# A new opening for a two-layer attention and expert kernel: order and size of the loads, the first two units ahead of the beats, the input norms moved to ACT

## The reference, cut to what matters

```python
x = x + L0_xattn(layernorm(x), ctx, mask, ...)   # cross attention, self attention, FFN
x = x + L0_ffn(layernorm(x), ...)                # shared expert + 8 routed experts, top 2
x = x + L1_xattn(layernorm(x), ctx, ...)         # two-way attention with a gate
x = x + L1_ffn(layernorm(x), ...)                # 8 experts that choose their tokens
# in L0_xattn, twice (ctx, then x itself): 16 heads of 8
q, k, v = x @ qw + qb, ctx @ kw + kb, ctx @ vw + vb
probs = softmax(q k^T / sqrt(8) + mask)
x = layernorm((probs v) @ ow + ob + x) * g + be
```

## Time and profile before

| | us |
|---|---|
| median of 3 runs | 1150.47 (1150.16 to 1150.87) |
| the profiled execution, its own time | 1151.73 |
| its span in the trace | 1149.9 |
| PE / DVE / ACT / POOL busy | 992.2 / 701.5 / 567.3 / 461.7 |
| mean granted TensorE clock (share of full speed) | 0.918 |

### The profile page before, as it was taken

How to read it: one execution, slowest core, us unless ns; L and a number is a source line. 1 busy time by engine, 2 the same in 40 slices (tenths; PEclk the granted TensorE clock), 3 DMA queues, 4 the chain that set the end, 5 groups by cost and what they waited for, 6 DMA issues and landing times.

```text
span 1149.9 us, 23311 instructions
## 1 busy us (share of the span) xinstructions
PE 992.2 (86%) x8694; PEld 776.5 (68%) x8694; DVE 701.5 (61%) x2226; ACT 567.3 (49%) x1286; POOL 461.7 (40%) x720
## 2 busy tenths in 40 slices
PE   3688888788888889988989999988997898898998
PEld 2365655566566556767887888766776686687877
DVE  4557676777767777567685333365788458356241
ACT  3366767676666756633233333223342653645453
POOL 4234454656757574475452000122454434313010
PEclk8678988978887979999999999998998999998999
DMA  8533443222222212000001333300000241330421
GB/s 192 161 99 93 125 139 96 67 70 58 84 62 79 70 47 79 10 12 9 6 4 36 91 112 90 106 17 14 19 23 15 55 127 25 71 93 19 143 60 56
DMA packets 71649, 78.59 MB, mean 68 GB/s; under 512 B 8325, under 2 KB 63732, under 8 KB 71408
## 3 DMA queue, kind: packets, MB, share of 16 engines
q1 hardware_dynamic: 66576, 70.02, 21.8%
q0 software_dynamic: 4096, 6.84, 2.7%
q10 hardware_dynamic: 864, 0.24, 0.1%
HBM read 38.25 MB, written 11.68 MB: 43 GB/s over the span
## 4 chain that ended last, share of the span: by engine, by line
PE 52%; DVE 21%; ACT 9%; POOL 9%; issue 6%; DMA 2%; SPq 1%; DVEq 0%; POOLq 0%; ACTq 0%
PE pb L1012 5%; PE pb L1002 4%; PE pb L754 4%; PE pb L839 3%; PE pb L826 3%; PE pb L828 3%; DVE arena L1143 3%; DVE XB L1108 3%; PE pb L711 3%; PE pb L602 3%; POOL arena L1851 2%; PE pb L745 2%; PE pb L746 2%; PE pb L703 2%; DVE arena L1098 2%
## 5 line engine op out<-in xcount | busy, mean ns | idle before, releaser
L1603 ACT ACTIVATE arena<-pb 77x512 f32<-77x512 f32 (+1 forms) x256 | 139.1, 599 | 81.6 <-PE pb L585 81.1
L1143 DVE TENSOR_REDUCE arena<-pb 128x4 f32<-128x308 f32 (+1 forms) x256 | 136.0, 575 | 61.7 <-PE pb L569 61.5
L1975 POOL DMA_INDIRECT arena<-yd,arena x64 | 63.8, 997 | 141.8 <-issue 141.8
L1658 ACT ACTIVATE arena<-pb 128x256 f32<-128x256 f32 x128 | 49.0, 385 | 143.0 <-PE pb L746 136.8
L1849 POOL TENSOR_SCALAR arena<-arena 128x4 f32<-128x4 f32 x64 | 12.8, 201 | 258.4 <-DVE arena L1101 256.7
L602 PE MATMUL pb<-arena 77*32 77x128 f32 (+1 forms) x2048 | 94.7, 310 | 0.0
L569 PEld LDWEIGHTS pb<-arena 64*128 64x128 bf16 x1024 | 30.9, 103 | 78.9 <-DVE arena L1143 33.8
L569 PE MATMUL pb<-arena 64*128 64x77 bf16 (+1 forms) x1024 | 51.1, 227 | 35.0 <-DVE arena L1143 21.2
L745 PE MATMUL pb<-XLT,arena 128*128 128x256 f32 x256 | 78.7, 389 | 2.1 <-DVE arena L1298 2.1
L746 PE MATMUL pb<-XLT,arena 128*128 128x256 f32 x256 | 77.5, 385 | 0.0
L1905 POOL DMA_INDIRECT xd<-XB,arena x64 | 63.8, 996 | 30.0 <-issue 19.6
(11 more groups left out here) (223 smaller groups left out, 2416.9 us busy)
## 6 DMA issues: line engine op xcount, KB each, us to landing
arena<-arena SPq DMA_DIRECT2D x190, 128.0 KB, 2.4
arena<-in_pe SPq DMA_DIRECT2D x32, 514.5 KB, 3.6
arena<-in_pr SPq DMA_DIRECT2D x8, 768.0 KB, 4.9
arena<-arena SPq DMA_DIRECT2D x46, 77.0 KB, 2.2
xd<-arena SPq DMA_DIRECT2D x8, 320.0 KB, 3.1
arena<-xd SPq DMA_DIRECT2D x8, 320.0 KB, 5.5
yd<-arena SPq DMA_DIRECT2D x8, 320.0 KB, 5.2
XO<-in_x SPq DMA_DIRECT2D x8, 256.0 KB, 4.0
```

Of the source, the lines that this page charges most:

```text
L1143: e.tensor_reduce(NM[i % 2][0][:, b, 4 * h:4 * h + 4, h2], bk[B + h2][:, 0:4 * nk].rearrange("p (t k) -> p t k", t=4), AX, ALU.max, negate ...
L1603: e.activation(PT[n % 2][0:nk, 512 * hf:512 * hf + 512], bk[2 + hf][0:nk, :], ACT.Exp, scale=SC8).then_inc(a_exp, 1)
```

## The change

- The opening's work for units 0 and 1 stands ahead of the beat loop on each engine, and `BEAT0` becomes -11. Unit 1's chain follows straight after unit 0's; `prep` is gone.
- Loads: x0, constants, the first half of `pa` (weights of cross attention and the biases, 516 columns; the packing is reordered for it), the context of group 0 alone, x1; then ones and zeros of unit 0, context of group 1, ones and zeros of unit 1, then the parts. The first four `rows` (512 columns) come amid unit 1's parts. The context of groups 2 and 3, x3 and the second half of `pa` come after unit 1's parts; ones of unit 2 at beat 0, the other 9 rows at beat 5, the rest of the context at beat 7.
- ACT issues the mask, and of units 0 and 1 the middle key parts and the mask slot, of unit 1 also the low key part.
- A semaphore `d_k0` counts unit 0's key parts alone, and ACT waits for it before it writes unit 1's queries over the buffer (before: all of unit 0's slots).
- The input norms: POOL computes the negated product of mean and inverse root too (`ln_scale_shift`, 8 instructions in place of 6), ACT applies with scale and bias (4 activations in place of DVE's 4). For groups 3 to 7 the apply stays in its beat, at the end of ACT's part.
- The bias folding starts at beat -4 (transposes) and -3, 0 (products); DVE's parts stand at -3, -1 and 1. `values(1)` goes behind `s1(7)` at beat -4.

The diff, cut to its core:

```diff
-BEAT0, BEAT1 = -24, NCH + 32
+BEAT0, BEAT1 = -11, NCH + 32
 def first(i):
-    return {1: -21, 2: -13}.get(i, 8 * i - 22)
+    return 8 * i - 22 if i > 2 else BEAT0
+def rests(i, x):
+    return 4 * i + ((1, 3, 2, 4) if i < 2 else (1, 2, 3, 4))[x]
...
 # SP
+            e.dma_start(CST[:, :], cst).then_inc(d_cst, 16)
+            e.dma_start(pa[:, 0:516], A["pa"][:, 0:516]).then_inc(d_wa, 16)
+            e.dma_start(ctg(0), A["ctxT"][:, 0:GB * C]).then_inc(d_ct[0], 16)
+            load_x(1)
+            L.wait_ge(v_cst, 2)
+            ones_rows(0)
+            spread_open(0)
+            e.dma_start(ctg(1), A["ctxT"][:, GB * C:2 * GB * C]).then_inc(d_ct[1], 16)
+            ones_rows(1)
+            spread_open(1)
+            L.wait_ge(a_f, 2)
+            spread_k(0, 1, (0, 3, 5))
+            load_x(2)
+            L.wait_ge(a_f, 4)
+            spread_q(0, 1, (0, 1, 2))
+            L.wait_ge(g_rest, rests(0, 2))
+            spread_k(0, 3, (2,))
+            L.wait_ge(a_mid, 2)
+            spread_q(0, 2, (3, 4))
+            L.wait_ge(g_rest, rests(0, 3))
+            spread_q(0, 3, (5,))
+            L.wait_ge(a_f, 6)
+            spread_k(1, 1, (0, 3, 5))
+            e.dma_start(rows[:, 0:512], A["rows"][:, 0:512].to_broadcast([128, 512])).then_inc(d_rows, 16)
...
+            e.dma_start(CT[:, 2 * GB * C:4 * GB * C], A["ctxT"][:, 2 * GB * C:4 * GB * C]).then_inc(d_ct[0], 16)
+            load_x(3)
+            e.dma_start(pa[:, 516:], A["pa"][:, 516:]).then_inc(d_wa, 16)
...
 # PE, ahead of the beats
+            keys(0)
+            ta(0)
+            queries(0)
+            values(0)
+            keys(1)
+            ta(1)
+            queries(1)
...
 # ACT, ahead of the beats
+            def ln_apply(kind, x, dst, src):
+                s = lns[kind][x % 2]
+                L.wait_ge(g_y[kind], x + 1)
+                for b in range(GB):
+                    ins = e.activation(dst[:, b, :], src[:, b, :], ACT.Identity, bias=s[:, 44 + b:45 + b],
+                                       scale=s[:, 36 + b:37 + b])
+                ins.then_inc(v_ap[kind], 1)
...
+            ln_apply(LN0, 0, grp(XB, 0), grp(XO, 0))
+            open_keys(0)
+            turned(5, 0, (p_ta, 1), a_xt)
...
+            middle(0, (g_rest, rests(0, 0)), GB * C)
+            open_queries(0)
+            ln_apply(LN0, 1, grp(XB, 1), grp(XO, 1))
+            middle(1, (g_rest, rests(0, 1)), 512)
+            L.wait_ge(a_mid, 1)
+            spread_part(0, 2, (1, 4))
+            spread_mask(0)
+            turned(5, 1, (p_ta, 2), a_xt)
+            open_keys(1)
+            va(0)
+            L.wait_ge(d_k0, 96)
+            open_queries(1)
...
 # DVE, in the beats
-                    if kind == "c" and n == {0: -20, 1: -17, 2: -11}.get(i, 8 * i - 21):
-                        ln_apply(LN0, g, grp(XB, g), grp(XO, g))
 # ACT, in the beats
+                    if kind == "c" and i > 1 and n == first(i) + (i > 2):
+                        ln_apply(LN0, g, grp(XB, g), grp(XO, g))
...
 # POOL, ahead of the beats
+            ln_scale_shift(LN0, 0)
+            ln_scale_shift(LN0, 1)
+            for i in range(2):
+                rest(2 * i, (a_f, 4 * i + 2), g_rest, GB * C)
+                rest_mid(2 * i, (a_mid, 2 * i + 1), (g_rest, rests(i, 0)), g_rest, GB * C)
+                rest(2 * i + 1, (a_f, 4 * i + 4), g_rest, 512)
+                rest_mid(2 * i + 1, (a_mid, 2 * i + 2), (g_rest, rests(i, 1)), g_rest, 512)
+                if i == 0:
+                    ln_scale_shift(LN0, 2)
```

241 lines of the change are left out of this document (145 added, 96 removed).

## The result

| | before | after |
|---|---|---|
| median of the runs beside each other | 1150.67 (1150.16 to 1155.57) | 1139.81 (1137.03 to 1145.37) |
| profiled execution, and its span | 1151.73, 1149.9 | 1145.37, 1143.6 |
| granted clock, mean over the span | 0.918 | 0.918 |
| first scores, first part product `s2(0)` | 25.97, 42.06 | 22.21, 34.37 |

The account below looks back on a forecast made before the run. The kernel was taken as PE-bound with stalls, its opening bound by bytes and SP's issues. Opening 6.9, biases 2.3 and norms 6.2 sum to 15.4 us, less 1 given back: 1136.0 us, own range 1132 to 1139, 8-in-10 range 1130.5 to 1142.5.

Parts of the forecast that it names:

- the opening: Before the first beat: reordered loads and issues bring `s2(0)` from 42.06 to 35.2 us, 6.9 us won.
- the biases: Beats 1 and 3: product and addition a beat apart remove waits of DVE and PE; 2.3 us, between 0 and 2.5.
- the norms: Input-norm applies of groups 3 to 7 moved off DVE to ACT: 6.2 us won, between 2 and 9.
- rival (a): Opening wins only 3.2 us, unit 1 held by ACT's queue or POOL's scales; 11.7 us in all, 1139; chance 0.17.
- Unit 0: In the opening: SP's shorter queue of issues brings first scores at 22.8 in place of 25.97, 3.2 us.
- Unit 1 and `s2(0)`: Later opening: last transfer landed at 30.9, maxima issued after 32.3, first part product at 35.2; 6.9 us in all.
- what costs nothing: Loads moved to beats 0, 5 and 7, 1.2 MB at the latter two, fit a DMA 0.4 to 0.3 busy.
- The 1 us for what is given back: Shortened beats find the next wait, such as the landing of the maxima; 1 us taken off 15.4.
- Rival (e): PE's clock falls to 0.66 for a hundred us between 60 and 500 us; slower, 1164; chance 0.03.
- (b): Opening as forecast, but the norms win nothing because ACT is late in those beats; 9.2 us, 1142; chance 0.12.
- (c): Each of four more transfers delays the chain by a 2.80 us landing; 11.2 us go, 1147; chance 0.03.
- (d): Unit 0 as late as before, opening gives 0, biases and norms half; 4 us, 1146 to 1148; chance 0.05.

Follow-up runs that it names:

- the repeat: The changed kernel run again without edit, in another session beside the kernel before: 1161.68 us, ratio 0.9920.
- the two pairs: Profiled kernels before and after: first 1151.73 and 1145.37 us; second, the kernel before profiled in a later session and the repeat (1161.68 us median).
- the undoing runs: Changed kernel with 1.3 MB of loads ahead of unit 0's last parts again (1160.28 us), or SP issuing all parts of units 0 and 1 (1139.58).
- the smaller transfers: Changed kernel with the constants in two transfers and the first weights in four, same bytes: 1144.81 us, one execution.

## Why the prediction was right, point by point

In short: the opening was right in mechanism and size, the biases were right in mechanism, and the norms had a wait behind them that was not foreseen. That the sum came near is partly luck, since the errors have opposite signs; the repeat's 9.4 us (5.3 to 13.5) lies below the 14.5 that the forecast of 1136.0 meant. The first measured median, 1139.8, is nearer to rival (a)'s 1139 than to the forecast, though the trace refutes (a).

**Unit 0: right, for the reasons given.** First scores at 22.21 where 22.8 was forecast; 3.8 us won where 3.2 was. The apply on ACT was mis-sized: 1.65 us, not 1.1. The row I went by was one 128-column activation of 0.28 us from PSUM with f32 output; the new ones read SBUF, with scale and bias per partition, and at 16 later places have a mean of 485 ns. The Trainium skill has this price, page "ScalarE: Activation LUTs", section "What ACT_TABLE_LOAD costs": by its figures an activation with two per-partition operands and 128 columns takes about 480 ns, and each that follows overlaps the one before by some 93, an estimate of 1.64 us for four; the rows agree. The longer apply cost nothing here, because ACT stood idle for 2.14 us later on, at 13.38, until POOL, which had the scale of group 1 in front, had made `rest(0)` (L2002). This is the loss that the prediction had walked (`middle(0)` done at 13.84, forecast 13.9). The staging of the queries followed it:

```profile
13.38 0.46 ACT L1687 ACTIVATE arena<-arena 128x308 bf16<-128x308 f32 x1 [2.14 <-POOL arena L2002]
13.75 1.25 ACT L1683 ACTIVATE arena<-pb,arena 128x512 f32<-128x512 f32 x2
...
17.19 1.15 POOL L2008 TENSOR_TENSOR arena<-arena 128x512 bf16<-128x512 f32 x1 [0.96 <-ACT arena L1687]
```

Low parts ended at 18.34 (forecast 18.8), the last issue stood at 18.83 (20.0). ACT's and POOL's chain set the time up to the staging's end at 15.0 (forecast 15.7), and from 15.02 SP issued its seven transfers back to back, one each 0.64 us, as walked; the last took 3.34 us to land, not 2.8.

**Unit 1 and `s2(0)`: right.** Last part landed at 31.0 (30.9), issue of the maxima 31.48 (32.3), `s2(0)` 34.37 (35.2). Won: 7.7 and 6.5 us in the two pairs, forecast 6.9. By the undoing runs some 2.9 us of it hang on the bytes and 3.0 to 3.5 on the parts that ACT issues; the two need not add up, since they share SP's queue and the DMA.

**The biases: right in mechanism, and in the size of the waits.** 2.3 us were forecast from the waits of PE alone; undoing it brought back 2.7 us of them. Beats 0 to 3 grew by 4.8 us, the rest being PE at a clock of 0.76 for 1.00, which the forecast had not counted and which was gone again by beat 8 (2.2). Whether the lower clock follows from the waits was not tested. Nor is it shown that the 2.3 us reach the end.

**The norms: the step that failed.** 6.2 us were forecast. The places were right: beats 20 and 36 won 2.3 us each (2.4 forecast), beats 21 and 37 another 1.0 and 1.2 that were not forecast, and in beats 52 and 68, where ACT was late, nothing came (0.6 forecast in all; 4.73 us before and 4.78 after, 4.76 and 4.74). For group 3, forecast at 0.8, the run that undoes the norms loses 1.4 us in beat 4 and wins 1.2 back in beat 5. The wait for ACT that the earlier trace rows show is still there in the kernel after:

```profile
187.59 0.40 PE L619 MATMUL pb<-arena 64*128 64x128 bf16 x8 [1.83 <-ACT arena L1667]
```

What was missed is what comes two beats later. The timeline of the kernel after, beats 19 to 22:

```profile
87.71 1.65 ACT L1657 ACTIVATE XB<-XO,arena 128x128 f32<-128x128 f32 x4
89.78 0.38 DVE L1151 BATCH_NORM_AGGREGATE arena<-arena 128x2 f32<-128x6 f32 x4
89.86 1.27 POOL L2085 TENSOR_TENSOR XB<-XB,rows 128x512 f32<-128x512 f32 x1
91.22 0.28 POOL L1948 TENSOR_SCALAR arena<-arena 128x4 f32<-128x4 f32 x1
93.79 1.11 DVE L1158 TENSOR_SCALAR XB<-XB,arena 128x128 f32<-128x128 f32 x4 [1.85 <-POOL arena L1958]
95.64 0.33 PE L720 MATMUL pb<-CST,arena 128*128 128x128 f32 x1 [1.86 <-DVE arena L1241]
```

DVE has the statistics of the attention norm ready at 90.16, but POOL reaches them at 91.22. It still has the addition of the bias (L2085) to do, and the two new instructions (0.5 us) and the low parts of the next unit (2.27 us) run in front of that. Before the change POOL had the same low parts in front, but DVE, held up by its own apply, came later still: POOL stood 3.08 us waiting for DVE's statistics there. So DVE waits 1.85 us and PE 1.86 (before 0.81 and 0.71). Of 4.6 us won in beats 20 and 36, 2.4 go back in 22 and 38. The gain of beats 21 and 37 makes up for that, and what eats the rest lies behind: beats 23, 24 and 39 lose 1.4, 0.6 and 0.6 us and beats 29 to 31 1.8, and in all of these stretches PE stands at its low clock for longer than before. In the prediction's words, POOL's half microsecond more per norm was counted only against ACT's `exp`; it should have been followed to the next norm on POOL's own queue.

The waits of PE from 60 to 500 us show the whole exchange, in us in total, times, longest. Kernel before:

```profile
PE pb L684 <- DVE arena L1185: 16.0, 13, 3.0
PE pb L569 <- DVE arena L1143: 15.4, 28, 1.4
PE pb L585 <- ACT arena L1603: 7.5, 6, 1.8
...
PE pb L623 <- DVE arena L1185: 2.9, 3, 1.2
...
PE pb L569 <- DMA arena<-arena: 1.6, 1, 1.6
```

Kernel after:

```profile
PE pb L603 <- DVE arena L1196: 14.1, 25, 1.4
PE pb L720 <- DVE arena L1241: 11.3, 12, 1.9
PE pb L619 <- ACT arena L1667: 9.6, 8, 1.8
...
PE pb L658 <- DVE arena L1241: 6.1, 4, 2.4
...
PE pb L603 <- DMA arena<-arena: 5.1, 5, 1.8
```

Before `to`, 4.7 us of waiting went, and before `s1` 1.3. In their place 2.1 us came for ACT, 3.2 before the turning of the normed x (L658, 6.1 us in four waits, all from 292 us on, whose cause I did not follow up), and 3.5 for DMAs, so that behind 60 us PE waits no less in sum than before. (The window from 60 us on starts at beat 5 before and at beat 9 after, so the two lists don't hold quite the same beats.) Of the waits for DMAs, the first scores of units 3, 5 and 7 have 1.50, 1.81 and 1.32 us, for their parts; the second of these is the line

```profile
117.14 0.44 PE L603 MATMUL pb<-arena 64*128 64x77 bf16 x8 [1.81 <-DMA arena<-arena]
```

The section on what costs nothing had named a wait of this kind as the price of a lost cover. But the loads that the change moved can't be what is felt here: the last of them, the rest of the context, was issued at 51.71 and had landed at 56.6, long before unit 5's parts. The issue isn't late either: in both kernels SP issues the same ten transfers for a unit's parts in the same order there, the last at 113.01 after and at 126.30 before, in each case over a us after POOL made it. It lands 4.1 us after its issue in the kernel after and 2.4 us in the kernel before, where the DMA share is no lower (0.71 from 126.3 to 128.8 us, against 0.60 and 0.50 from 113 to 117.2). Why that one transfer took longer is open. The share of the stretch did not rise (0.27 after, 0.28 before), so a mean share says nothing of what a single transfer waits for.

What the norms are worth in all is not pinned down: undoing them in the changed kernel costs 4.4 us (2.7 to 9.1), doing them alone on the kernel before gives 2.2 by the medians with an interval that takes in nothing and 6.8. Values of 2.7 to 6.8 us fit both, so in the whole time even the 6.2 forecast is not excluded. What did fail, seen in the beats, is the step that let the gain of beats 20 and 36 pass on unshortened.

**The 1 us for what is given back** was too little. The prediction's own term for it had no row behind it. In its place the traces show 2.4 us before `to` in beats 22 and 38 and 3.5 of waits for parts, and 0.6 not won in beats 52 and 68. Taken off the 15.4 that leaves 8.9, with 2.2 of beats 21 and 37 added 11.1. The repeat gave 9.4 and the first measurement 12.8. This is reckoning after the fact, with the clock left out.

**The clock.** Rival (e) did not happen as a loss, though one of the prediction's signs of being wrong did show, a clock below 0.87 from 60 to 500 us: it was 0.86. Another sign of being right, applies of 1.1 us, did not. The clock goes with more of the spread between executions than any edit here moves. Taking the time at the low one of its two levels (1.2 and 2.4 GHz) as twice the missing share of the mean clock times the span, the kernel before loses 0.33 us per us of it over 35 executions of one session (correlation 0.90), 0.36 over 25 of another (0.90), 0.44 over 11 (0.94), and the changed kernel 0.37 over 12 (0.92). These are correlations: a wait can lengthen the time and lower the clock together, and no run sets the clock by itself. I used 0.36 in the table above. Behind beat 0 the profiled kernel before stood low for 166.5 us and the one after for 174.1; 7.6 x 0.36 = 2.7 us. So the lead of the profiled pair, 6.4 us, is 9.1 set right for the clock behind beat 0. That leaves out the opening, where the low time was 21.2 us before and 13.7 after and PE mostly idled; over the whole span both traces have the same 187.7 us, and by that measure nothing would be set right. The profiled execution of after is the slowest of its four, with the lowest clock, which speaks for the first reckoning but doesn't prove it. The single edits, read in part from beats and in part from whole times (2.9 for bytes, 1.5 to 2.2 for biases, 0 to 4.4 for norms, and 3.6 that the opening lacks to 6.5), add up to 8 to 13 us. That doesn't contradict 9.4 and 12.8, but it is no proof, since the bytes don't show in the whole time.

**The other rivals.** (a), the opening wins 3.2 alone: refuted by 34.37. (b), the norms win nothing: not refuted on the kernel before, refuted in the changed one by the run that undoes them, and ACT was not the reason for what was lost. (c): refuted at 8 to 11 us by the smaller transfers. The fixed cost of about 2 us that the prediction set beside it is given by the Trainium skill, page "DMA: Bandwidth & Descriptors", section "Anatomy of one DMA", for transfers issued from GpSimd; all of these are issued by SP and ACT. (d): refuted for the opening by 22.21 and 34.37 and for the biases by the waits.

## What to carry to other kernels

Follow the chain of an opening instruction by instruction over all queues: that gave 22.8, 30.9, 32.3 and 35.2 us for what came at 22.2, 31.0, 31.5 and 34.4. When work moves off a busy engine, follow also the idle engine that feeds it to its next customer, two or three steps on, and read no promise from a mean busy share of the DMA for a transfer with a due time. Compare two kernels by their own executions of one session before calling overlapping ratios a draw. Where the granted clock goes with most of the spread from run to run, compare single beats and medians, and trust no single trace to a few microseconds.
